# Two gather loops of a graph network on one Trainium2 core: index, edge and time loads per round of four chunks, one-hots of the first layer made in other instructions, the bound on counts tested in the setup

## The chip, the cores and the metric

The kernel runs on one core of a Trainium2 chip. The metric is the device time of one execution in microseconds (us). A core has five engines that run their own instruction streams and meet at semaphores: TensorE (PE, matrix products), VectorE (DVE), ScalarE (ACT), GpSimd (POOL, which also issues the indirect gathers here) and SyncE (SP, which issues DMAs). ACT issues DMAs too. A capital name with a q (SPq, DVEq) is the part of an engine that issues instructions.

## What is computed

Four graph layers over 6,250 nodes of 128 features and E = 206,250 edges, sorted by destination. Each layer is added to the running node features x after a normalisation. Only the first two layers and the setup are changed:

```
h = relu(layernorm(x))                      # before each layer
# layer 0: gated relational messages, one of 8 weights per edge
msg = (h @ W[rel])[src] * edge_weight1 * sigmoid((h @ g[rel])[src])
x = x + relu(segment_sum(msg, dst))
# layer 1: edge network with a time gate
ef  = (relu(attr @ We1 + be1) @ We2 + be2) * sigmoid(time * Wt + bt)
msg = relu(concat(h[src], ef) @ Wn1 + bn1) @ Wn2 + bn2
x = x + segment_sum(msg, dst) + h
# layers 2 and 3: a GRU layer and three graph convolutions, whose sums over
# edges are products with a 6250 x 6250 matrix of edge counts
```

The count matrix (how often an edge goes from node s to node d) is made beside layer 0, as bf16, for layers 2 and 3. A bf16 number holds whole counts exactly up to 256, so the kernel has a flag: if a count is larger, a branch makes the rest of the digits.

## The kernel before

Edges are padded to 206,848 = 101 rounds of NB = 4 chunks of CH = 512 edges, a chunk being J = 4 tiles of 128 edges. There are 404 chunks.

**Setup** (lines 270 to 434). SP loads destinations by row and by column, sources and edge types (lines 306 to 310); DVE finds the least destination of each chunk and its span, SP stores that as `meta` and reads it back (lines 312 to 318), DVE computes keys and, in a loop of eight (lines 412 to 423), the first and last tile of each group. The last thing is that SP stores `gout` (line 327) and reads it back as `record` (line 329).

**Layer 0** (lines 572 to 730), a software pipeline over chunks, with a loop per engine. SP copies 4 columns of `idx8`, a tile in SBUF, to a slot `staged[:, b, :]`, also in SBUF, once per chunk (line 597), as soon as the four gathers that read that slot one round earlier have landed (`rows_in[b]`, line 602). POOL waits for the slot and for `chunk_done` of four chunks earlier, and issues four indirect gathers of 128 rows of 512 bytes (line 613). DVE makes a one-hot of 4 x 64 destinations per chunk (`one_hot`, line 180); ACT multiplies it by the edge weight in place, tile by tile (`weigh_chunk`, line 688); PE multiplies rows and one-hot (line 160, four products that sum into one window), and DVE adds the window to `acc` (line 201) and raises `chunk_done` (line 225).

Into the same loops the count matrix is woven, two groups per chunk for the first 98 rounds. For each group DVE computes eight numbers (line 520) and makes four pairs of one-hots in bf16: `lo_hot` of 128 (line 516) and `hi_hot` of 392 columns (line 517), in the order lo, hi, lo, hi; PE multiplies each pair (line 549) into one of four banks; ACT copies the bank to `block_out` (line 696) and makes a second pass over it, Relu(count - 256) with a sum (line 698), into `over[:, g]`. After the layer the maximum of `over` gives the flag (lines 775 and 794 to 798).

The order on DVE in each chunk is: two sets of keys, the one-hot of the next chunk, the one-hots of two groups, then the wait for this chunk's window (`close_window`, line 206). The order on PE is: wait for rows, window product, first group, second group.

**Layer 1** (lines 938 to 1156), again a loop per engine. SP loads per chunk the 4 index columns (line 993, from `src_idx` in SBUF), and per two chunks a 256 KB piece of edge attributes from HBM (line 997). ACT issues per chunk a 256 KB load of times, broadcast to 128 partitions (line 1070). POOL gathers (line 1014). PE makes four products (lines 1041, 1047, 1059 and 160, with counts of edge types at 163), ACT makes `tw`, `hid` and `msg` (lines 1085, 1090, 1096), DVE makes `ef` (1140), `z` (1153), the one-hots (1129, 180) and adds the window (199, 201). The gather into a slot waits for `z` of four chunks earlier (line 1011).

```
                            sp.wait_ge(rows_in[b], base + 16 * J * o)
                            load(b, o * NB + b)
```

are the two lines of layer 0's loop on SP by which a slot is filled again.

## Time and profile before

| | |
|---|---|
| time, median of 3 runs | 7884.42 us (7872.66 to 7892.95) |
| profiled execution | 7896.64 us, of which 7894.2 us are the span of the trace |
| PE, DVE, ACT, POOL busy | 72%, 40%, 29%, 40% of the span |
| setup | 0 to 166 us |
| layer 0 with the count matrix | 321 to 2972 us |
| layer 1 | 3069 to 5858 us |
| layers 2 and 3 | 5858 us to the end |
| DMA | 811.20 MB in 460919 packets; 218904 of them under 512 B |

An idle stretch of an engine is printed ahead of the instruction that ended it, as [us <-what released it]. "issue" means that the trace shows nothing that the engine waited for, "remote" that a semaphore was waited for whose last increment the trace doesn't tie to an instruction that ended just then.

### The profile page before, as it was taken

Reading aid. Unit: us, or ns where it says so; the run is one execution under the profiler, and the core shown is the slowest. Engines: PE = TensorE matmul, PEld = TensorE weight load, DVE = VectorE, ACT = ScalarE, POOL = GpSimd, SP = SyncE. Lnnn points to the kernel's source line nnn. Section 1 sums busy time; section 2 is a strip of 40 time slices with the busy share of each in tenths; the row PEclk is TensorE's granted clock in tenths of the full one; section 3 lists DMA queues with packets and bytes.
Section 4 is the critical chain, followed back from the end, with each engine's and each line's share of the span. In section 5 each row is a group of like instructions: output and inputs, shape, how many; then the busy total and the mean of one; then the engine's idle time right before and its main releaser. Section 6 shows DMA issues by size and latency. Waiting matters only on the chain. (4 is left out here: it accounts for less than half of the span.)

```text
span 7894.2 us, 105906 instructions
## 1 busy us (share of the span) xinstructions
PE 5657.7 (72%) x25772; PEld 3387.9 (43%) x25773; DVE 3166.8 (40%) x11018; ACT 2317.7 (29%) x5705; POOL 3138.5 (40%) x3263
## 2 busy tenths in 40 slices
PE   0766666566666654777777777777786996999999
PEld 0333333333333433444444444444453453444444
DVE  6566666666666654333333333333322112000000
ACT  0244444444444442232222222222211112111100
POOL 0265565556665562555555555555530000000000
PEclk9856555665656556777777777777767998999999
DMA  1322222222222222333333333333313443555555
GB/s 49 147 73 73 73 72 57 73 73 73 74 73 73 69 69 72 97 96 97 94 95 96 96 95 98 95 94 97 96 53 117 157 129 131 191 173 194 172 193 162
DMA packets 460919, 811.20 MB, mean 103 GB/s; under 512 B 218904, under 2 KB 233266, under 8 KB 457671
## 3 DMA queue, kind: packets, MB, share of 16 engines
q1 hardware_dynamic: 285148, 407.76, 16.6%
q0 software_dynamic: 103968, 213.28, 10.3%
q10 hardware_dynamic: 71728, 189.18, 7.4%
q8 instruction: 45, 0.74, 0.0%
q14 instruction: 30, 0.25, 0.0%
HBM read 697.44 MB, written 110.80 MB: 102 GB/s over the span
## 5 line engine op out<-in xcount | busy, mean ns | idle before, releaser
L613 POOL DMA_INDIRECT e_rows<-scratch_table,e_staged x1616 | 1583.3, 980 | 1364.1 <-DVEq L225 607.1
L1014 POOL DMA_INDIRECT e_rows<-scratch_table,e_staged x1616 | 1533.9, 949 | 1342.5 <-DVE e_z L1153 707.6
L549 PE MATMUL e_banks<-hi_hot,lo_hot 128*128 128x392 bf16 x3138 | 1073.0, 494 | 704.4 <-remote 314.4
L517 DVE TENSOR_SCALAR hi_hot<-iota_hi,key 128x392 bf16<-128x392 f16 x3138 | 1078.9, 344 | 16.7 <-issue 16.5
L160 PE MATMUL e_win<-e_onehot,e_msg 128*128 128x64 f32 x3232 | 562.3, 332 | 663.1 <-ACT e_msg L1096 645.9
L160 PEld LDWEIGHTS e_win<-e_onehot,e_msg 128*128 128x128 f32 x3232 | 542.6, 247 | 968.7 <-ACT e_msg L1096 825.5
L160 PE MATMUL e_win<-e_onehot,e_rows 128*128 128x64 f32 x3232 | 683.6, 386 | 282.1 <-issue 212.4
L549 PEld LDWEIGHTS e_banks<-hi_hot,lo_hot 128*128 128x128 bf16 x3138 | 354.7, 132 | 1227.4 <-issue 534.0
L160 PEld LDWEIGHTS e_win<-e_onehot,e_rows 128*128 128x128 f32 x3232 | 696.4, 306 | 413.7 <-issue 366.3
L516 DVE TENSOR_SCALAR lo_hot<-iota_lo,key 128x128 bf16<-128x128 bf16 x3138 | 783.3, 250 | 193.4 <-remote 156.0
L1324 PE MATMUL c_sums<-ring,parts 128*128 128x512 bf16 (+1 forms) x3822 | 789.8, 368 | 80.9 <-DMA c_bias<-in_conv_b 80.9
L1096 ACT ACTIVATE e_msg<-e_z 128x512 f32<-128x512 f32 x404 | 254.4, 630 | 1891.3 <-DVE e_z L1153 1530.4
L1059 PE MATMUL e_p<-wn1b,e_ef 128*128 128x128 f32 x3232 | 614.4, 348 | 0.0
L1548 POOL DMA_DIRECT2D c_w<-in_convT x3 | 1.6, 534 | 1444.8 <-POOLq L65 1444.8
L1324 PEld LDWEIGHTS c_sums<-ring,parts 128*128 128x128 bf16 x3822 | 361.7, 98 | 489.9 <-DMA c_bias<-in_conv_b 81.5
L1059 PEld LDWEIGHTS e_p<-wn1b,e_ef 128*128 128x128 f32 x3232 | 520.1, 245 | 31.5 <-DVE e_ef L1140 0.9
L1047 PE MATMUL e_p<-e_hid,we 128*128 128x512 f32 x808 | 506.5, 713 | 1.1 <-ACT e_hid L1090 0.8
L1612 DVE SCALAR_TENSOR_TENSOR c_y<-c_pO,dinv,c_bias 128x128 f32<-128x128 f32 x147 | 41.6, 345 | 1118.2 <-PE c_pO L1574 1118.2
L688 ACT ACTIVATE e_onehot<-e_onehot,weight 128x64 f32<-128x64 f32 x1616 | 429.2, 342 | 149.2 <-DVE e_onehot L180 102.1
L1140 DVE SCALAR_TENSOR_TENSOR e_ef<-e_p,cols,e_tw 128x512 f32<-128x512 f32 x404 | 302.5, 749 | 389.8 <-PE e_p L1047 241.5
L698 ACT ACTIVATE excess<-e_banks,limit 128x392 bf16<-128x392 f32 x784 | 456.1, 582 | 0.0
L1153 DVE TENSOR_TENSOR e_z<-e_p,e_rows 128x512 f32<-128x512 f32 x404 | 279.4, 692 | 431.2 <-PE e_p L1059 203.7
(188 smaller groups left out, 5767.1 us busy)
## 6 DMA issues: line engine op xcount, KB each, us to landing
ring<-scratch_counts SPq DMA_DIRECT2D x336, 896.0 KB, 4.7
e_time<-in_time_rows ACTq DMA_DIRECT2D x404, 256.0 KB
e_rows<-scratch_table,e_staged POOLq DMA_INDIRECT x3232
e_edge<-in_edge_T SPq DMA_DIRECT2D x202, 256.0 KB
scratch_counts<-h ACTq DMA_DIRECT2D x12, 3136.0 KB
scratch_counts<-type_mem ACTq DMA_DIRECT2D x12, 3136.0 KB
scratch_table<-table_tile SPq DMA_DIRECT2D x49, 512.0 KB, 2.6
e_staged<-idx SPq DMA_DIRECT2D x404, 2.0 KB
```

Source lines behind the costliest of these rows:

```text
L160: last = nc.tensor.matmul(win[:, 0:W], rows[:, j, :], onehot[:, j, :], start=(j == 0), stop=(j == J - 1))
L516: nc.vector.tensor_scalar(lo_hot, iota_lo[:, :], key[:, 0:1], None, ALU.is_equal)
L517: return nc.vector.tensor_scalar(hi_hot, iota_hi[:, :], key[:, 1:2], None, ALU.is_equal)
L549: return nc.tensor.matmul(bank, lo_hot[:, slot, :], hi_hot[:, slot, :], start=start, stop=stop)
L613: pool.indirect_dma_start(rows[:, b, j, :], None, A["table0"], bass.IndirectOffsetOnAxis(ap=staged[:, b, j:j + 1], axis=0),).then_inc(rows ...
L688: last = nc.scalar.activation(onehot[:, half, j, :], onehot[:, half, j, :], ACT.Copy, scale=weight0[:, bass.ds(c * J + j, 1)])
L698: nc.scalar.activation(excess[:, k % 2, :], bank, ACT.Relu, bias=limit[:, 0:1], accum_out=over[:, bass.ds(g, 1)]).then_inc(s["flushed"], 1)
L1014: pool.indirect_dma_start(rows[:, b, j, :], None, A["table1"], bass.IndirectOffsetOnAxis(ap=staged[:, b, j:j + 1], axis=0),).then_inc(rows ...
L1047: nc.tensor.matmul(p2[:, (b - 1) % 2, :], we2[:, :], hid[:, (b - 1) % 2, :], start=True, stop=True).then_inc(s["p2"], 1)
L1059: last = nc.tensor.matmul(p3[:, (b - 2) % 2, j * P:(j + 1) * P], ef[:, (b - 2) % 2, j * P:(j + 1) * P], wn1b[:, :], start=True, stop=True)
L1140: nc.vector.scalar_tensor_tensor(ef[:, k, :], p2[:, k, :], cols1[:, 1:2], tw[:, k, :], ALU.add, ALU.mult).then_inc(s["ef"], 1)
L1324: last = nc.tensor.matmul(to, parts[part][:, bass.ds(t, 1), :], counts, start=(start and part == 0), stop=(stop and part == 2))
```

## The change

1. **Layer 0, loads.** `staged` holds two halves of 16 columns; SP fills one half per round (101 copies of 64 bytes per partition in place of 404 of 16), two rounds ahead, as soon as all four chunks of the round before last have landed. POOL waits for indexes once per round.
2. **Layer 0, edge one-hot.** DVE makes each of its four tiles in one instruction with compare and multiply; ACT's `weigh_chunk` goes.
3. **Layer 0, count matrix.** The four `lo_hot` of a group are made by one `tensor_tensor` of 512 columns ahead of the four `hi_hot`. ACT's second pass goes.
4. **The bound.** In the setup the destinations are loaded again, shifted by 256 edges (`later`), and compared: an edge whose destination equals that of the edge 256 places on sets the flag.
5. **Layer 1, loads.** SP loads per round: 16 index columns, four chunks of edges (512 KB), four chunks of times (1 MB, before on ACT's queue). The tiles for edges and times move into `h`. At the start two rounds are loaded ahead of `type_i`.

```
-            def make_pair(key, lo_hot, hi_hot):
-                nc.vector.tensor_scalar(lo_hot, iota_lo[:, :], key[:, 0:1], None, ALU.is_equal)
+            def make_lows(size, key, lo_hot):
+                return nc.vector.tensor_tensor(lo_hot, iota_lo[:, :].unsqueeze(1).to_broadcast([P, size, P]),
+                                               key[:, :, 0:1].to_broadcast([P, size, P]), ALU.is_equal)
...
+        def open_weighted_window(s, c, onehot, weight):
+            for j in range(J):
+                last = nc.vector.tensor_scalar(onehot[:, j, :], iota_w[:, :], dst_rel[:, bass.ds(c * J + j, 1)],
+                                               weight[:, bass.ds(c * J + j, 1)], ALU.is_equal, ALU.mult)
+            last.then_inc(s["onehot"], 1)
...
+                    pool.memset(later[:, :], float(2 * NP)).then_inc(s_far, 1)
...
                     sp.dma_start(rel[:, :], A["rel_cols"]).then_inc(s_rel, 16)
+                    sp.wait_ge(s_far, 1)
+                    sp.dma_start(later[0:full, :], flat_dst[LIMIT:LIMIT + full * span]
+                                 .rearrange("(p e) -> p e", e=span)).then_inc(s_later, 16)
...
                     nc.vector.tensor_copy(gout[:, 0, :], gfirst[:, :]).then_inc(s_gout, 1)
+                    dve.wait_ge(s_later, 32)
+                    nc.vector.memset(over[:, :], 0.0).then_inc(s_repeat, 1)
+                    nc.vector.tensor_tensor(repeats[:, :], dst_rows[:, :, :].rearrange("p t e -> p (t e)"), later[:, :],
+                                            ALU.is_ge).then_inc(s_repeat, 1)
+                    dve.wait_ge(s_repeat, 2)
+                    nc.vector.tensor_reduce(over[0:ROUNDS, :], repeats[:, :], AXX, ALU.max).then_inc(s_repeat, 1)
...
# layer 0, SP
-                    with sp.Fori(1, ROUNDS) as o:
-                            sp.wait_ge(rows_in[b], base + 16 * J * o)
-                            load(b, o * NB + b)
+                    def load(half, r):
+                        sp.dma_start(staged[:, half, :], idx8[:, bass.ds(r * (NB * J), NB * J)]).then_inc(index_in[half], 16)
+
+                    def reload(half, r):
                         for b in range(NB):
+                            sp.wait_ge(rows_in[b], base + 16 * J * (r - 1))
+                        load(half, r)
+                    load(0, 0)
+                    load(1, 1)
+                    reload(0, 2)
+                    with sp.Fori(1, (ROUNDS - 1) // 2) as o:
+                        reload(1, 2 * o + 1)
+                        reload(0, 2 * o + 2)
...
# layer 0, ACT
-                        nc.scalar.activation(excess[:, k % 2, :], bank, ACT.Relu, bias=limit[:, 0:1],
-                                             accum_out=over[:, bass.ds(g, 1)]).then_inc(s["flushed"], 1)
-                                if k % 2 == 0:
-                                    weigh_chunk(h * (GPH // 2) + i * NB + k // 2 + 1, (k // 2 + 1) % 2)
...
# after layer 0
-                    nc.vector.tensor_reduce(top[:, :], over[:, :], AXX, ALU.max).then_inc(s["top"], 1)
...
# layer 1, SP
+                def load(half, r):
+                    sp.dma_start(staged[:, half, :], src_idx[:, bass.ds(r * (NB * J), NB * J)]).then_inc(index_in[half], 16)
+                    sp.dma_start(edge_in[:, half, :, :], A["edge_T"][bass.ds(r * NB, NB), :, :]
+                                 .rearrange("(q a) k e -> (a k) q e", a=2)).then_inc(edges_in[half], 16)
+                    sp.dma_start(time_in[:, half, :, :].rearrange("p b e -> p (b e)"),
+                                 A["time_rows"].rearrange("(r b) e -> r (b e)", b=NB)[bass.ds(r, 1), :]
+                                 .to_broadcast([P, NB * CH])).then_inc(times_in[half], 16)
+
+                def reload(half, r):
+                    for b in range(NB):
+                        sp.wait_ge(rows_in[b], base + 16 * J * (r - 1))
...
+                    sp.wait_ge(s["p1"], (r - 1) * NB)
+                    sp.wait_ge(s["tw"], (r - 1) * NB)
+                    load(half, r)
+                load(0, 0)
+                load(1, 1)
                 sp.dma_start(type_i[:, :], A["type_cols"]).then_inc(s["type_in"], 16)
...
# layer 1, ACT
-                        load_time(c + NB - 1, b + NB - 1)
```

## Rows read from the trace of the kernel before

**Rows 1.** Busy time by stretch; columns are length, engines, PEclk, DMA share, GB/s.

```profile
166.00:321.00 155.00, 103.66 (x343) 53.60 (x343) 97.77 (x126) 37.73 (x116) 0.00 (x0) 0.96 0.42 166
321.00:2972.00 2651.00, 1677.34 (x6370) 1022.68 (x6370) 1715.24 (x7870) 1221.50 (x3968) 1583.30 (x1616) 0.59 0.24 70
3069.00:5858.00 2789.00, 2030.81 (x9696) 1355.74 (x9696) 926.42 (x2426) 808.91 (x1211) 1533.91 (x1616) 0.76 0.35 95
```

**Rows 2.** Groups by line, 321 to 2972 us: busy us, mean ns, idle before.

```profile
L613 POOL DMA_INDIRECT e_rows<-scratch_table,e_staged x1616 | 1583.3, 980 | 1364.1 <-DVEq L225 607.1 <-issue 450.6 <-DVEq L657 306.4
```

**Rows 3.** Who waited, 321 to 2972 us, DVE: total us, times, longest.

```profile
DVE acc L201 <- remote: 421.1, 152, 10.6
...
DVE lo_hot L516 <- remote: 156.0, 41, 8.4
```

**Rows 4.** Timeline of layer 0: start us, duration, instruction, idle before.

```profile
1845.17 0.21 DVE L201 TENSOR_TENSOR acc<-acc,e_win 128x64 f32 x1
...
1847.78 0.48 SPq L597 DMA_DIRECT2D e_staged<-idx  x1
...
1850.19 0.94 POOL L613 DMA_INDIRECT e_rows<-scratch_table,e_staged  x1 [0.30 <-issue]
...
1853.29 0.22 DVE L201 TENSOR_TENSOR acc<-acc,e_win 128x64 f32 x1 [3.82 <-remote]
```

**Rows 5.** Groups by line, 3069 to 5858 us.

```profile
L1014 POOL DMA_INDIRECT e_rows<-scratch_table,e_staged x1616 | 1533.9, 949 | 1342.5 <-DVE e_z L1153 707.6 <-issue 528.4 <-DMA e_staged<-src_idx 106.5
...
L1153 DVE TENSOR_TENSOR e_z<-e_p,e_rows 128x512 f32<-128x512 f32 x404 | 279.4, 692 | 431.2 <-PE e_p L1059 203.7 <-remote 139.6 <-issue 84.8
...
L199 DVE TENSOR_TENSOR type_mem<-type_mem,e_win 16x64 f32 x404 | 84.3, 209 | 836.8 <-remote 406.4 <-PE e_win L163 406.1 <-issue 24.3
```

**Rows 6.** Timeline of layer 1.

```profile
4503.88 0.49 SPq L993 DMA_DIRECT2D e_staged<-src_idx  x1
...
4504.72 0.28 SPq L997 DMA_DIRECT2D e_edge<-in_edge_T  x1
...
4505.39 0.28 PE L163 MATMUL e_win<-e_onehot,e_oh_type 128*16 128x64 bf16 x4
...
4509.28 0.21 DVE L199 TENSOR_TENSOR type_mem<-type_mem,e_win 16x64 f32 x1 [3.88 <-remote]
...
4509.83 0.69 DVE L1153 TENSOR_TENSOR e_z<-e_p,e_rows 128x512 f32<-128x512 f32 x1 [0.21 <-issue]
4510.44 0.22 DVE L1129 TENSOR_TENSOR e_oh_type<-iota_w,type_f 128x64 bf16<-128x64 f32 x1
```

**Rows 7.** Timeline of DVE in layer 0, for the spacing of starts.

```profile
1848.76 0.31 DVE L517 TENSOR_SCALAR hi_hot<-iota_hi,key 128x392 bf16<-128x392 f16 x1
1848.99 0.24 DVE L516 TENSOR_SCALAR lo_hot<-iota_lo,key 128x128 bf16<-128x128 bf16 x1
1849.15 0.31 DVE L517 TENSOR_SCALAR hi_hot<-iota_hi,key 128x392 bf16<-128x392 f16 x1
...
1854.24 0.52 DVE L180 SCALAR_TENSOR_TENSOR e_onehot<-dst_rel,neg_w,iota_w 128x256 f32<-128x256 f32 x1
1854.68 0.24 DVE L516 TENSOR_SCALAR lo_hot<-iota_lo,key 128x128 bf16<-128x128 bf16 x1
```

**Rows 8.** Timeline of the setup.

```profile
160.26 0.31 SPq L327 DMA_DIRECT2D scratch_groups<-gout  x1
...
166.09 6.69 DVE L115 TENSOR_REDUCE mean<-x 128x49 f32<-128x6272 f32 x1 [5.85 <-PEq L65]
```

**Rows 9.** Timeline of the start of layer 1.

```profile
3061.30 0.34 SPq L999 DMA_DIRECT2D type_i<-in_type_cols  x1
...
3074.57 0.93 DVE L1115 TENSOR_SCALAR type_f<-type_i 128x1616 f32<-128x1616 int32 x1
```

**Rows 10.** DMA issues of the page: line, queue, count, size of one.

```profile
e_time<-in_time_rows ACTq DMA_DIRECT2D x404, 256.0 KB
...
e_edge<-in_edge_T SPq DMA_DIRECT2D x202, 256.0 KB
```

More of the change, by code:

```diff
@@ L294, in bass_gnn @@
                                                           ("rows", "cols", "src", "rel", "x", "w"))
+                s_far, s_later, s_repeat = (sem(st, f"setup_{n}") for n in ("far", "later", "repeat"))
                 s_low, s_high, s_span, s_meta_out, s_meta_in, s_base_in, s_ready, s_id = (
@@ L531, in group_vector @@
                 dve.wait_ge(s["taken"], g + 1)
+                make_lows(PAIRS, key[:, half, :, :], lo_hot[:, half * PAIRS:(half + 1) * PAIRS, :])
                 for j in range(PAIRS):
-                    last = make_pair(key[:, half, j, :], lo_hot[:, half * PAIRS + j, :], hi_hot[:, half * PAIRS + j, :])
+                    last = make_high(key[:, half, j, :], hi_hot[:, half * PAIRS + j, :])
                 last.then_inc(s["made"], 1)
@@ L586, in bass_gnn @@
                 s = {n: sem(st, f"e0_{n}") for n in WINDOW_SEMS +
-                     ("taken", "made", "keyed", "flushed", "copied", "limit", "y_keyed", "y_made", "y_taken")}
-                index_in = [sem(st, f"e0_index{b}") for b in range(NB)]
+                     ("taken", "made", "keyed", "flushed", "y_keyed", "y_made", "y_taken")}
+                index_in = [sem(st, f"e0_index{k}") for k in range(2)]
                 stored = [sem(st, f"e0_stored{k}") for k in range(2)]
@@ L725, in _ @@
                     block_of(whole, 0, GROUPS - whole * GPH, 16 * (whole // 2))
-                    for c in range(GROUPS // 2 + 1, NC):
-                        weigh_chunk(c, c % 2)
                     act.wait_ge(stored[0], 16 * (whole // 2 + 1))
@@ L975, in run_steps @@
                     for b in range(SPR):
-                        step(o * SPR + NB + b, b, False)
+                        step(o * SPR + NB + b, NB + b, False)
                 load_meta(NC - SPR)
@@ L999, in _ @@
-                sp.dma_start(type_i[:, :], A["type_cols"]).then_inc(s["type_in"], 16)
-                for b in range(NB):
-                    load(b, b, None)
-                with sp.Fori(1, ROUNDS) as o:
-                    for b in range(NB):
-                        load(b, o * NB + b, o)
+                def load(half, r):
[5 more added lines that the diff above has]
+                                 .to_broadcast([P, NB * CH])).then_inc(times_in[half], 16)
@@ L1006, in _ @@
+                reload(0, 2)
+                with sp.Fori(1, (ROUNDS - 1) // 2) as o:
+                    reload(1, 2 * o + 1)
+                    reload(0, 2 * o + 2)
             @block.gpsimd
             def _(pool):
-                def gather(b, c, o, first):
-                    pool.wait_ge(index_in[b], o * 16 + 16)
-                    if not first:
-                        pool.wait_ge(s["z"], c - (NB - 1))
-                    pool.sem_inc(s["begun"], 1)
-                    for j in range(J):
-                        pool.indirect_dma_start(
-                            rows[:, b, j, :], None, A["table1"],
-                            bass.IndirectOffsetOnAxis(ap=staged[:, b, j:j + 1], axis=0),
-                        ).then_inc(rows_in[b], 16)
@@ L1018, in _, with one_round @@
-                for b in range(NB):
-                    gather(b, b, 0, True)
-                with pool.Fori(1, ROUNDS) as o:
-                    for b in range(NB):
-                        gather(b, o * NB + b, o, False)
+                def one_round(half, r, before, first):
+                    pool.wait_ge(index_in[half], 16 * before + 16)
+                    for b in range(NB):
+                        if not first:
+                            pool.wait_ge(s["z"], r * NB + b - (NB - 1))
+                        pool.sem_inc(s["begun"], 1)
+                        for j in range(J):
+                            pool.indirect_dma_start(
+                                rows[:, b, j, :], None, A["table1"],
+                                bass.IndirectOffsetOnAxis(ap=staged[:, half, b * J + j:b * J + j + 1], axis=0),
+                            ).then_inc(rows_in[b], 16)
@@ L1024, in _ @@
+                one_round(0, 0, 0, True)
+                with pool.Fori(0, (ROUNDS - 1) // 2) as o:
+                    one_round(1, 2 * o + 1, o, False)
+                    one_round(0, 2 * o + 2, o + 1, False)
             @block.tensor
```

112 lines of the change are left out of this document (49 added, 63 removed).

## The prediction

> **What bounds the kernel now.** I read the stages first. Layer 0 takes 2651 us and layer 1 takes 2789 us, and neither is filled by an engine: in layer 0 PE is busy for 1677, DVE for 1715 and POOL for 1583 us, in layer 1 PE for 2031 and POOL for 1534 us [rows 1]. Something waits in both, so the groups and waits come next.
>
> POOL sets the pace from below. A gather takes 0.98 us in layer 0 and the next starts 0.30 us later [rows 2, 4], so a chunk of four needs 4 x 1.28 = 5.12 us; in layer 1 it needs 4 x (0.95 + 0.30) = 5.0 us [rows 5]. For 404 chunks that is 2068 and 2020 us. Above this pace POOL waits 607.1 us for `chunk_done` of DVE in layer 0 and 707.6 us for `z` of DVE in layer 1 [rows 2, 5]. These two sums are what can be won in the loops at most.
>
> DVE in turn waits in layer 0 for "remote": 421.1 us in 152 waits ahead of the window's addition and 156.0 us in 41 waits ahead of `lo_hot`, together 577 us in 193 stalls of 3.0 us [rows 3]. In layer 1 it is 406.4 + 139.6 = 546 us [rows 5]. One stall of each layer shows what it is. In layer 0 DVE adds a window at 1845.17, has made its last one-hot at 1849.46 (4.29 us of work), and then waits 3.82 us, to 1853.29 [rows 4, 7]. POOL had issued its last gather at 1850.19. SP had issued the copy of the index columns at 1847.78, 5.5 us before the stall ends. In layer 1 the products of the window are done 0.28 us after 4505.39, but DVE gets their semaphore at 4509.28 after 3.88 us; SP had copied indexes at 4503.88, 5.4 us before [rows 6]. The same 5.4 to 5.5 us in two loops that share only this copy on SP and the gathers is my evidence that **the small copies from SBUF to SBUF hold back semaphores** that others wait for. There are 404 copies and 193 stalls in layer 0: about one stall for two copies.
>
> **The change, part by part.** The sum starts from the profiled execution, 7896.6 us.
>
> *Copies per round, layer 0.* 404 copies become 101, each still 128 rows, of 64 bytes in place of 16. Their number is taken to count, not their bytes. With one stall for each, 101 x 3.0 = 303 us of waiting remain of POOL's 607.1: **-304 us**. The bounds are 0 (the copies are not the cause) and -607 (no stall is left, POOL's own pace remains).
>
> *Copies per round, layer 1.* Likewise 202 pairs of copies, 707.6 / 202 = 3.5 us each, become 101: 354 us remain, **-354 us**, with bounds 0 and -708. The loads of times leave ACT's queue for SP's: per round 2 x 256 KB of edges and 4 x 256 KB of times follow the index copy [rows 10], 1.57 MB, at the 166 GB/s that the stretch ahead of layer 0 moved [rows 1] 9.5 us of a round of about 24 us. They are asked for a whole round ahead of their use, so a late arrival is hidden by that round. Queued behind SP's new waits (four gathers, `p1`, `tw`) is only the next round's load; PE, ACT and POOL wait for that a round later. What the bytes do to the stalls is a rival below.
>
> *The weighted one-hot.* DVE's one instruction for 4 x 64 columns is followed by the next after 0.44 us; four small ones, at the 0.16 us that `lo_hot` takes to the next start [rows 7], are 0.64 us: +0.20 us per chunk, up to +0.48 if they take 0.23 us each as `hi_hot` does. *Merged lows.* Four `lo_hot` cost 4 x 0.16 = 0.64 us. Not in the trace of before is a `tensor_tensor` of 512 bf16 columns with broadcast operands. The nearest is `z`, 512 columns, f32, next start after 0.61 us [rows 6]: -0.03 us per group. From 128 to 392 columns the fast form adds only 0.07 us, 0.27 ns per column [rows 7]; at that pace 512 columns would be 0.26 us, -0.38 per group; the other end is z's whole duration of 0.69 us, +0.05. I take z's spacing, as it too reads two tensors. DVE's work per chunk is then 4.29 + 0.20 - 0.06 = 4.43 us (3.7 to 4.9), under POOL's 5.12: **0**, hidden behind the gathers. Where that cover is gone the net 0.14 us costs 404 x 0.14 = 57 us.
>
> [...]
>
> *ACT* loses the weighing (a hop between DVE and PE) and the second pass over every bank. It was busy for 1222 of 2651 us [rows 1] and its share is not the pace; banks come free earlier. 0 taken, a few us either way.
>
> *Setup.* A further 0.8 MB on SP's queue goes ahead of the store of `meta`; at 166 GB/s [rows 1] it is 5 us: **+5** (0 to +8), since DVE's next step waits for that round trip. On POOL a fill of 2048 columns goes first, beside loads that last far longer. DVE's comparison and maximum of 2048 columns, at z's spacing of 0.61 us for 512 [rows 6], take 2.4 us each. They run after `gout`, while SP stores and reads back the groups, from 160.26 to DVE's next start at 166.09 [rows 8]: hidden; 4.8 us if not. The reduction left out after layer 0 saves about 1 us; 0 taken.
>
> *Start of layer 1.* `type_i` now waits behind two rounds of loads, 3.1 MB, at 166 GB/s 19 us; it is issued at 3061.30 and used at 3074.57, 13 us later, with two fills of DVE in between [rows 9]. About **+8** (0 to +15).
>
> Sum: 7896.6 - 304 - 354 + 5 + 8 = 7252 us. The median of the runs is 12 us below the profiled execution, so the forecast is **7240 us**.
>
> **The rivals.**
>
> *The stalls go altogether.* If a round's copy is issued while there is slack, POOL is four chunks ahead and never notices: -607 - 708 in place of -304 - 354, 6583 us; with a part of the slack, anything from there to 7100. For it: DVE's 4.43 us is below 5.12 us, so a lag could be made up, at 0.7 us per chunk about as much as a stall of 3 us costs in four chunks. [...]
>
> *The stall grows in layer 1.* The 1 MB of times and the edges follow the copy on the same queue. If the stall lasts as long as the queue's transfers, 7.0 us in place of 3.5 us, one stall costs as much as two did, and the layer gains nothing: 7240 + 354 = 7594 us. For it: 9.5 us of transfer per round. Against: the edge load of 256 KB, issued 0.84 us behind the copy, doesn't lengthen that stall beyond 5.4 us, what layer 0 shows without one [rows 4, 6]. [...]
>
> *The copies are not the cause, and DVE becomes the bound of layer 0.* Then the remote waits stay, and what DVE does in a chunk lies on the path: ahead of each wait for PE's semaphore stands +0.20 us for the one-hot and, at the upper end, +0.05 us for each of the two merges. At the lower value, without a gain from the merge, 404 x 0.20 = 81 us, with setup and start 94 us: 7884 + 94 = 7978 us. It decides from the point where the copies' gain in both layers is under 94 us. For it: gathers, too, are in flight in each stall, and their traffic doesn't change. Against: the 5.4 us.
>
> *Nothing that can be told from no change*, 7884 us: gains and costs cancel.
>
> **How the numbers follow.** The forecast, one stall per round, 0.45 (its own range 7100 to 7400); stalls gone in good part, below 7100, 0.20; layer 1 without gain, 7400 to 7650, 0.20; slower, about 7980, 0.10; no change, 0.05. About 0.3% is what a measurement of this kernel can tell from no change. The range 6650 to 7650 leaves out the last two and the lowest end of the second, under 0.2 together. Faster 0.85, same 0.05, slower 0.10.
>
> **What would show it.** Right: in layer 0 the remote waits of DVE halve, to about 100 stalls and 300 us, POOL's wait for `chunk_done` to about 300 us, and each stall that is left ends some 5.4 us after a copy on SP; the like in layer 1 with `z` and 354 us. If POOL's wait falls under 100 us, the first rival holds. If layer 1's stalls are few but 7 us long, the second. If their number stays near 193 and 404 chunks take over 2651 us, the third. The merged lows should start 0.6 us ahead of the first `hi_hot`, the setup should end 5 us later. The prediction is most wrong if the number of copies is not what counts but, say, what they read or who issues them.

## The result

The changed kernel takes **7753.1 us** (median of 4 runs, 7751.8 to 7755.9), the kernel before 7880.4 us (4 runs, 7872.7 to 7893.0). The ratio is 0.9835 with a 95% interval of 0.9823 to 0.9846: 127 us faster, where 640 were forecast, and outside of the range, which ended at 7650. The profiled execution of the changed kernel has a span of 7749.6 us; all its rows here come from it.

There is a second result, which the first measurement could not show. The experiments ran on several chips. On two of them (before: 7839 and 7915 us) the kernel before takes about as long as on the first, and the kernels profiled there with all their gathers have the same waits. On four others the kernel before takes 6593 to 6597 us, and there **the changed kernel is slower**: 6752.1 us against 6595.0, ratio 1.0237 (1.0220 to 1.0254). What parts the two kinds in the traces is the wait that they call "remote": every kernel with all its gathers has it on the one kind, and none has it on the other. I call them chips with and without stalls. Each ratio below is to the kernel before on the same chip. That the chip decides is not shown: only one of them was used at two times (without stalls at both), and one of ten runs of `lo32`, on a chip where the other nine took 6598 to 6613 us at a granted clock of 0.85, took 7833 us at 0.63; it has no trace, and it is left out of what follows.

The stretches of the changed kernel, on the first chip (columns as in [rows 1]: length, busy time of PE, PEld, DVE, ACT, POOL, granted clock, DMA share, GB/s):

```profile
168.00:324.00 156.00, 102.27 (x343) 52.90 (x343) 98.28 (x125) 37.69 (x116) 0.00 (x0) 0.97 0.41 165
324.00:2853.00 2529.00, 1557.37 (x6371) 937.07 (x6371) 1791.45 (x6732) 381.59 (x784) 1749.24 (x1616) 0.66 0.24 73
2950.00:5738.00 2788.00, 2035.12 (x9789) 1355.47 (x9790) 916.88 (x2426) 775.22 (x1210) 1524.97 (x1607) 0.77 0.30 94
```

Compared with [rows 1], the gain lies in layer 0, which went from 2651 to 2529 us. Layer 1, where 354 us were forecast, stays (2789 and 2788). One column moved that nothing in the prediction moves: POOL's busy time in layer 0, 1583 to 1749 us for the same 1616 gathers. These are POOL's groups, to be compared with [rows 2] and [rows 5]. The columns are busy us, mean ns, and idle time before by what ended it; the first row is layer 0, the second layer 1:

```profile
L647 POOL DMA_INDIRECT e_rows<-scratch_table,e_staged x1616 | 1749.2, 1082 | 1074.1 <-issue 477.0 <-DVEq L693 308.2 <-DVEq L232 288.9
```

```profile
L1045 POOL DMA_INDIRECT e_rows<-scratch_table,e_staged x1607 | 1525.3, 949 | 1215.8 <-DVE e_z L1174 722.6 <-issue 493.2
```

In layer 0 POOL waits 289 us for `chunk_done` (DVEq L232) where it waited 607, so the 304 us that were forecast for its waiting are there, nearly to the number; but each gather takes 1082 ns where it took 980, and that gives 166 us back. In layer 1 the wait for `z` is 723 us after and 708 before: there are a quarter of the copies and the same waiting.

DVE's waits for remote, layer 0 and layer 1 (total us, times, longest):

```profile
DVE acc L208 <- remote: 221.6, 111, 7.3
DVE lo_hot L542 <- remote: 99.4, 45, 8.1
```

```profile
DVE type_mem L206 <- remote: 404.0, 91, 8.3
...
DVE e_z L1174 <- remote: 253.7, 102, 4.2
```

In layer 0 they fell from 577 to 321 us [rows 3], in layer 1 they rose from 546 to 658 [rows 5]. The stall itself can be seen where no copy is near. The timeline of layer 0 of the changed kernel:

```profile
1811.01 0.95 POOL L647 DMA_INDIRECT e_rows<-scratch_table,e_staged  x1 [0.30 <-issue]
1812.27 0.94 POOL L647 DMA_INDIRECT e_rows<-scratch_table,e_staged  x1 [0.30 <-issue]
...
1818.54 0.94 POOL L647 DMA_INDIRECT e_rows<-scratch_table,e_staged  x1 [0.30 <-issue]
```

```profile
1797.77 24.00 SPq L626 DMA_DIRECT2D e_staged<-idx  x2
```

```profile
1821.28 0.49 SPq L626 DMA_DIRECT2D e_staged<-idx  x1
```

```profile
1814.29 1.08 PE L161 MATMUL e_win<-e_onehot,e_rows 128*128 128x64 f32 x8 [2.80 <-issue]
```

```profile
1812.83 0.98 DVE L196 TENSOR_SCALAR e_onehot<-iota_w,dst_rel,weight 128x64 f32<-128x64 f32 x4
1813.73 0.68 DVE L542 TENSOR_TENSOR lo_hot<-iota_lo,key 128x512 bf16<-128x512 bf16 x1
1814.33 1.00 DVE L546 TENSOR_SCALAR hi_hot<-iota_hi,key 128x392 bf16<-128x392 f16 x4
...
1820.68 0.22 DVE L208 TENSOR_TENSOR acc<-acc,e_win 128x64 f32 x1 [3.82 <-remote]
```

PE has finished the window at 1815.37. DVE gets to know at 1820.68, 5.3 us later. SP issued one copy at 1797.77 and the next at 1821.28 (the first row groups the two, the second has the later one), 17.6 us before PE's last product and 0.6 us after the stall: none is issued in between. What is under way from 1811.01 to 1819.5 are seven gathers, one behind the other. In the kernel before, SP waited for the landing of gathered rows to issue its copy, and I had read the distance between copy and stall as a cause. It was read off one stall of each layer, and the whole trace of the kernel before does not have it as a rule. Of the 193 stalls of layer 0, counted there, 35 end 5.2 to 5.7 us after a copy was issued, and 122 end less than 1 us after one, too soon for that copy to have begun them; in layer 1 it is 83 of 227 that end at 5.2 to 5.7 us.

### The profile page after: what moved, and what is told of

Its sections match the earlier page's. It is cut to its first block and busy times, and to the rows that moved or that the text cites. A ratio compares the mean times of both kernels' runs of the same rounds, so it can differ in the third digit from the quotient of the medians.

```text
span 7749.6 us, 97114 instructions
## 1 busy us (share of the span) xinstructions
PE 5526.1 (71%) x25772; PEld 3281.9 (42%) x25773; DVE 3241.6 (42%) x9879; ACT 1444.4 (19%) x2521; POOL 3306.1 (43%) x3264
## 5 line engine op out<-in xcount | busy, mean ns | idle before, releaser
L647 POOL DMA_INDIRECT e_rows<-scratch_table,e_staged x1616 | 1749.2, 1082 | 1074.1 <-issue 477.0
L1045 POOL DMA_INDIRECT e_rows<-scratch_table,e_staged x1616 | 1533.8, 949 | 1316.3 <-DVE e_z L1174 722.6
L580 PE MATMUL e_banks<-hi_hot,lo_hot 128*128 128x392 bf16 x3138 | 983.9, 458 | 625.6 <-DVE hi_hot L546 340.6
L161 PE MATMUL e_win<-e_onehot,e_rows 128*128 128x64 f32 x3232 | 635.0, 364 | 355.5 <-issue 185.0
L161 PEld LDWEIGHTS e_win<-e_onehot,e_rows 128*128 128x128 f32 x3232 | 629.8, 282 | 492.9 <-issue 326.3
L546 DVE TENSOR_SCALAR hi_hot<-iota_hi,key 128x392 bf16<-128x392 f16 x3138 | 800.0, 316 | 0.0
L580 PEld LDWEIGHTS e_banks<-hi_hot,lo_hot 128*128 128x128 bf16 x3138 | 313.9, 121 | 1108.1 <-issue 617.1
L542 DVE TENSOR_TENSOR lo_hot<-iota_lo,key 128x512 bf16<-128x512 bf16 x786 | 536.1, 682 | 167.1 <-remote 99.4
L1072 PE MATMUL e_p<-h,we 64*128 64x512 f32 x808 | 347.8, 951 | 139.0 <-issue 119.4
L1345 PE MATMUL p3S<-ring,parts 128*128 128x512 bf16 (+1 forms) x1911 | 393.7, 368 | 68.7 <-DVE emb L1482 68.7
L206 DVE TENSOR_TENSOR type_mem<-type_mem,e_win 16x64 f32 x404 | 84.3, 209 | 811.1 <-remote 404.0
```

Of the source, the lines that this page charges most:

```text
L161: last = nc.tensor.matmul(win[:, 0:W], rows[:, j, :], onehot[:, j, :], start=(j == 0), stop=(j == J - 1))
L542: return nc.vector.tensor_tensor(lo_hot, iota_lo[:, :].unsqueeze(1).to_broadcast([P, size, P]), key[:, :, 0:1].to_broadcast([P, size, P]), ...
L546: return nc.vector.tensor_scalar(hi_hot, iota_hi[:, :], key[:, 1:2], None, ALU.is_equal)
L580: return nc.tensor.matmul(bank, lo_hot[:, slot, :], hi_hot[:, slot, :], start=start, stop=stop)
L647: pool.indirect_dma_start(rows[:, b, j, :], None, A["table0"], bass.IndirectOffsetOnAxis(ap=staged[:, half, b * J + j:b * J + j + 1], axis=0),
L1045: pool.indirect_dma_start(rows[:, b, j, :], None, A["table1"], bass.IndirectOffsetOnAxis(ap=staged[:, half, b * J + j:b * J + j + 1], axis=0),
```

## The experiments

Two theories stand against each other. COPIES is the prediction's: SP's small copies hold semaphores back. GATHERS: gathers in flight do it. A third, PORT, is about the 166 us of longer gathers: VectorE's comparisons hold POOL up.

**Twice the copies.** The suspected cost doubled:

```diff
 sp.dma_start(staged[:, b, :], idx8[:, bass.ds(c * J, J)]).then_inc(index_in[b], 16)
+sp.wait_ge(spare_in[b], 16 * o)
+sp.dma_start(spare[:, b, :], idx8[:, bass.ds(c * J, J)]).then_inc(spare_in[b], 16)
```

> The kernel before, with every per-chunk index copy on SP's queue issued a second time into a buffer that nobody reads (some 800 copies more in the two edge layers). Two theories. COPIES (the prediction's): the small copies on SP's queue hold back what TensorE reports; then twice as many would cost about what taking three quarters of them away was forecast to bring, 300 us or more, so 8200 us or later. GATHERS: TensorE's semaphore increments are held back while gathered rows are landing, and the copies only happened to be issued at that moment, since SP waits for the rows; then the second copies cost nothing, 7860 to 7910 us, and the acc wait for remote in layer 0 stays near 421 us.

6597.7 us, ratio 1.0001 (0.9992 to 1.0011). But the chip has no stalls, so this says that 808 more copies cost nothing there, not what they do on the other kind. It cannot settle the theories, and neither can the next two experiments, from the same chip.

**The loads per round, one layer at a time,** the kernel before otherwise:

> The kernel before with the index loads per round in layer 0 alone. COPIES: -300 us by the prediction, 7580 us. GATHERS: within 30 us of before; the 134 us that layer 0 gained in the whole change then come from the other parts (the weighing taken from ScalarE, the second pass taken off, the one-hots in another order).

> The kernel before with the loads per round of four chunks in layer 1 alone. COPIES: -350 us by the prediction, 7530 us. GATHERS: the copies are not the cause, so within 30 us of before, 7850 to 7910 us; the comparison of the two traces had layer 1 at 2772 to 2752 us.

Layer 0 alone: 6597.5 us, 1.0001 (0.9992 to 1.0011). Layer 1 alone: 6585.8 us, 0.9983 (0.9974 to 0.9993). The first moves nothing, the second some 10 us. On this chip there is nothing else to win, as POOL's group of `l0_only` shows (first layer 0, then layer 1):

```profile
L618 POOL DMA_INDIRECT e_rows<-scratch_table,e_staged x1616 | 1600.7, 991 | 795.9 <-issue 468.2 <-DVEq L666 303.7 <-DVEq L225 24.1
L1023 POOL DMA_INDIRECT e_rows<-scratch_table,e_staged x1616 | 1543.8, 955 | 594.4 <-issue 469.4 <-DMA e_staged<-src_idx 113.1 <-DVE e_z L1162 11.9
```

POOL waits 24 us for `chunk_done` where it waited 607 [rows 2] and 12 us for `z` where it waited 708 [rows 5]. It gathers without a break, from 318.9 to 2410.9 us in layer 0 and from 2514.0 to 4549.1 us in layer 1: POOL is the bound of both edge layers on a chip without stalls.

**One gather of four.** The kernel before, all of SP's copies kept, with only gather 0 of each chunk; three quarters of the rows stay zero, so that part of the sums is left out.

```diff
-for j in range(J):
+for j in range(1):
     pool.indirect_dma_start(rows[:, b, j, :], None, A["table0"], ...)
```

The arguments behind `...` are left out here. Not shown: the same in layer 1, the waits for rows at a quarter of their counts, and one fill of the rows with zeros ahead of each layer.

> The kernel before, with only the first of the four gathers of each chunk in both edge layers; the other three quarters of the rows stay zero, so the output is not the reference's. SP's copies are untouched. COPIES: the stalls stay, as each copy is still there: the waits for remote of VectorE stay near 700 us in layer 0 and 608 us in layer 1, and layer 1, which is not bound by GpSimd, stays at about 2790 us. GATHERS: the waits for remote fall to a quarter or less of that (under 150 us in each layer), layer 0 goes to VectorE's pace, 4.4 us a chunk or some 1850 us, and layer 1 falls by 300 us or more.

> The kernel before with one of four gathers of each chunk (the other rows stay zero, so the output is not the reference's), once more for a chip with waits for remote. There GATHERS: under 300 us of such waits on VectorE, and within 150 us of 6260 us. COPIES: the waits stay near 1190 us. On a chip without them: 6260 us, nothing told.

On three chips without stalls it took 6258, 6261 and 6260 us (one_gather, one_gather_2, one_gather_3), which tells only how much POOL's pace costs there. The fourth run met a chip with stalls, on which the kernel before took 7915 us (7 runs): **6261.4 us**, ratio 0.7912. That is the time of the other chips. DVE's waits in both edge layers of that run, 322 to 4210 us:

```profile
DVE type_mem L199 <- PE e_win L163: 323.5, 399, 1.6
DVE e_z L1157 <- PE e_p L1063: 269.5, 399, 1.7
DVE e_ef L1144 <- PE e_p L1051: 236.3, 221, 2.1
...
DVE acc L201 <- PE e_win L160: 22.6, 12, 4.1
```

No row of it says remote, and the waits for PE are no longer than 4.1 us, where single stalls had been up to 10.6 [rows 3]. On the same chip `skew`, described below, has 454 us of waits for remote in layer 0 alone. All 808 index copies are there. GATHERS holds and COPIES falls: the stalls need the gathers in number, a kernel with a quarter of them has none, and in layer 1 of the changed kernel a quarter of the copies left the waiting whole. Whether it is POOL's issuing of the gathers or the rows themselves on their way that holds semaphores back, this does not tell, as both went.

**The one-hots.** The changed kernel again on a chip without stalls, and four edits of it.

> The changed kernel itself, beside the kernel before on the chip of these experiments. On the chip of the first measurement, whose trace has 1190 us of waits for remote, it was 130 us faster than before (0.9835). Here the kernel before takes 6595 us and its traces have no wait for remote at all. COPIES: with no stall to remove nothing is left of the gain, and what is left is the removed weighing on ScalarE and its way to TensorE, 0.98 to 1.00. GATHERS: the copies never mattered, and the gain of 134 us in layer 0 came from the one-hots; GpSimd sets the pace of layer 0 here (1616 gathers of 980 ns), and the merged one-hots lengthen its gathers to 1082 ns, so no faster than before, 6550 to 6700 us.

> The changed kernel with the narrow one-hots not merged: for each tile the 128-wide and then the 328-wide comparison, as before. The prediction has the two forms equal (0.61 against 0.64 us a group). Theory PORT: four of the wide comparisons back to back hold GpSimd out of memory it shares with VectorE, and lengthen the gathers beside them; with the pairs back the mean gather of layer 0 falls from 1082 ns to about 980 ns, and the kernel is faster than the changed one by 60 to 160 us. Rival: the mean gather stays above 1050 ns and the time is the changed kernel's within 20 us.

The edit (the wide comparison has 392 columns, the 328 of that text is a slip):

```diff
-make_lows(PAIRS, key[:, half, :, :], lo_hot[:, half * PAIRS:(half + 1) * PAIRS, :])
 for j in range(PAIRS):
+    nc.vector.tensor_scalar(lo_hot[:, half * PAIRS + j, :], iota_lo[:, :], key[:, half, j, 0:1], None, ALU.is_equal)
     last = make_high(key[:, half, j, :], hi_hot[:, half * PAIRS + j, :])
```

> As the changed kernel, but the merged comparison is split into its four narrow comparisons, still ahead of the four wide ones. It tells the order from the form. PORT by order (wide comparisons back to back are what hurts): mean gather as in the changed kernel, near 1080 ns, in layer 0. PORT by form (the merged tensor-tensor comparison is what hurts): near 980 ns, as with the pairs.

> The changed kernel with the layer-0 node one-hot made by one VectorE comparison and weighed on ScalarE again, as before. The prediction put the change of this at +0.20 us a chunk of VectorE, hidden, 0 in the time. Theory: what the changed kernel gained in layer 0 comes from the way VectorE, ScalarE, TensorE that this puts back into each chunk (two semaphores less), so this is slower than the changed kernel by 50 to 130 us; rival: within 20 us of it, with the gain in the second pass over the counts.

The edit of `weigh_act` puts back `weigh_chunk` of the kernel before, word for word. The group of the gathers of layer 0 in each, in the order after_again, pairs, lows_first, weigh_act:

```profile
L647 POOL DMA_INDIRECT e_rows<-scratch_table,e_staged x1616 | 1767.1, 1093 | 801.1 <-issue 469.6 <-DVEq L693 308.9 <-DVEq L232 22.6
```

```profile
L647 POOL DMA_INDIRECT e_rows<-scratch_table,e_staged x1616 | 1698.4, 1051 | 800.9 <-issue 469.0 <-DVEq L693 308.8 <-DVEq L232 23.2
```

```profile
L648 POOL DMA_INDIRECT e_rows<-scratch_table,e_staged x1616 | 1804.8, 1117 | 800.4 <-issue 474.2 <-DVEq L694 308.2 <-DVEq L232 18.0
```

```profile
L650 POOL DMA_INDIRECT e_rows<-scratch_table,e_staged x1616 | 1647.9, 1020 | 802.2 <-issue 459.2 <-DVEq L696 310.1 <-DVEq L235 32.9
```

| kernel | time, us | ratio | POOL busy, layer 0 | first to last gather |
|---|---|---|---|---|
| l0_only (one-hots of before) | 6597.5 | 1.0001 | 1600.7 | 2092.0 |
| weigh_act | 6637.4 | 1.0063 | 1647.9 | 2139.2 |
| pairs | 6689.2 | 1.0141 | 1698.4 | 2189.6 |
| after_again | 6752.1 | 1.0237 | 1767.1 | 2258.3 |
| lows_first | 6790.4 | 1.0295 | 1804.8 | 2296.1 |

The last column is the one before it plus 491 us, in every row within 1 us. So **on a chip without stalls layer 0 lasts as long as its gathers, and what the one-hot edits cost is what they add to the gathers**. No other engine is needed to explain it: 1767.1 - 1600.7 = 166 us longer in POOL, 157 us longer in all. Undoing the merge gives 63 us back, undoing the weighing on DVE 115; together that is more than the 157, so the two do not simply add. lows_first kept the four narrow comparisons apart, yet bundled, and is the slowest: with these the order, not only the merged form, matters.

Several of the expectations missed. The changed kernel is slower than either theory had it (6700 us at most). `pairs` gained the 63 us at the low end of its range, but its mean gather fell to 1051 ns only, not to 980. `weigh_act` was expected to be slower than the changed kernel by 50 to 130 us and is faster by 115.

**Without the wide comparisons.** I had `hi_hot` in suspicion, four in a row:

> The changed kernel without the wide comparisons of layer 0: their tile is filled with zeros once, so the counts, and with them the output, are not the reference's; all else is issued as before. It tells whether these comparisons are what lengthens the gathers beside them. Theory PORT: every gather of layer 0 takes its 944 ns, beside the merged narrow comparison, the weighted slices and the window sums too, and on a chip without waits for remote layer 0 takes 1616 x (0.944 + 0.29) = 1994 us, against 2258 us in the changed kernel and 2092 us before: 6490 us in all. Rival: some other instruction beside them does it, then the mean stays above 1000 ns. On a chip with waits for remote: the mean falls likewise, and layer 0 keeps its waits for remote of 220 us or more.

6704.7 us, 1.0165 (1.0136 to 1.0195), mean gather 1060 ns, not 944: my theory had the wrong instruction, or at least not all of them. The timeline of DVE and POOL of that kernel shows another:

```profile
1000.05 1.04 DVE L196 TENSOR_SCALAR e_onehot<-iota_w,dst_rel,weight 128x64 f32<-128x64 f32 x4
1000.09 0.94 POOL L647 DMA_INDIRECT e_rows<-scratch_table,e_staged  x1 [0.30 <-issue]
...
1000.95 1.28 DVE L542 TENSOR_TENSOR lo_hot<-iota_lo,key 128x512 bf16<-128x512 bf16 x2
1001.34 1.72 POOL L647 DMA_INDIRECT e_rows<-scratch_table,e_staged  x1 [0.30 <-issue]
```

The gather beside the weighted slices takes its 0.94 us. The next is issued at 1001.34, within the first of two merged comparisons that end at 1002.23, and takes 1.72 us. The same is seen in the changed kernel on the first chip; this gather starts 0.31 us before a merged comparison ends:

```profile
1822.56 0.69 DVE L542 TENSOR_TENSOR lo_hot<-iota_lo,key 128x512 bf16<-128x512 bf16 x1
1822.94 1.35 POOL L647 DMA_INDIRECT e_rows<-scratch_table,e_staged  x1 [0.31 <-issue]
```

What counts is what DVE runs when a gather starts. This table sorts the 1616 gathers of layer 0 by that, worked out from the traces (number of gathers and their mean in ns; a narrow comparison is `lo_hot`, merged in the last two columns, a wide one `hi_hot`):

| DVE at the gather's start | l0_only | woven_2 | pairs | weigh_act | after_again |
|---|---|---|---|---|---|
| idle, keys or window sum | 496, 944 | 271, 944 | 478, 944 | 687, 944 | 500, 944 |
| edge one-hot | 84, 1050 | 328, 989 | 245, 953 | 136, 1068 | 358, 1003 |
| narrow comparison | 160, 1012 | 260, 956 | 500, 1164 | 437, 1172 | 637, 1275 |
| wide comparison | 876, 1007 | 757, 1013 | 393, 1099 | 356, 961 | 121, 1025 |

In `after_again` the gathers that start in a merged comparison make up 211 of the 242 us by which all gathers exceed 944 ns. In `weigh_act` they make up 100 us, and this difference of 111 us is nearly all of the 119 us between the two in POOL's busy time. The merged comparison is the same in both; with the weighing back on ScalarE fewer gathers start in it, and each of them loses less (0.23 us in place of 0.33). So an edit of DVE's instructions costs by where it lets the gathers fall among them. Why they fall where they do, and why one start costs more than another, the traces do not settle.

In `after_again` the 637 gathers that start in a merged comparison, which reads two tiles, take 1.275 us in the mean, against 0.944 us for those that start while VectorE is idle, at its keys or at a window sum; the one of 1.72 us above takes 0.78 us more than that. What such a gather waits for, no run shows; that it is held out of memory, as theory PORT has it, is my guess. In the other direction no such delay is seen. In the changed kernel on the first chip 664 of the 786 merged comparisons start while a gather is under way, and they take 682 ns in the mean, the 122 others 685. In the timeline under the result a gather starts first, and a merged comparison in the middle of it takes its usual 0.68 us:

```profile
1814.76 0.94 POOL L647 DMA_INDIRECT e_rows<-scratch_table,e_staged  x1 [0.30 <-issue]
1815.26 0.68 DVE L542 TENSOR_TENSOR lo_hot<-iota_lo,key 128x512 bf16<-128x512 bf16 x1
```

The four weighted slices cost most gathers beside them nothing: of the 358 that start in one in `after_again`, the median is 944 ns.

**The order.** The same instructions as in `pairs`, with the four slices put one by one behind every second pair (the edit in short, not word for word):

```diff
 for j in range(PAIRS):
     lo_hot(j); hi_hot(j)
+    if j % 2 == 1:
+        one weighted slice of the next node one-hot
```

> The changed kernel with pairs again and with the four weighted slices of the node one-hot put one by one behind every second pair, in place of four in a row ahead of the groups: the same instructions of VectorE as in the kernel called pairs, in another order. If what lengthens a gather is an unbroken run of two-byte comparisons beside it, the slices (beside which a gather took 944 ns) break the run, and the mean gather falls below that kernel's 1052 ns towards 1000 ns: 6610 to 6650 us on a chip without waits for remote. If only the total time of such comparisons counts, the mean stays at 1050 ns and the time at 6690 us.

> The kernel called woven again, to have it on a chip without waits for remote: there its gathers, 986 ns beside the pairs in its first run, give layer 0 1616 x (0.98 + 0.29) = 2052 to 2090 us, and 6575 to 6620 us in all, faster than the kernel called pairs (6689) by 70 us or more. On a chip with such waits again 0.992 of before.

```profile
L649 POOL DMA_INDIRECT e_rows<-scratch_table,e_staged x1616 | 1595.7, 987 | 799.4 <-issue 467.2 <-DVEq L695 307.3 <-DVEq L232 25.0
```

6587.0 us, 0.9987 (0.9977 to 0.9996): 102 us faster than `pairs` by order alone, through the gathers again (1051 to 987 ns), as the expectations had it or a little more. That an unbroken run of comparisons is what lengthens them is not shown, though: `l0_only` has the same eight pairs in one unbroken run, and its gathers take 991 ns. By the table above its 1036 gathers that start in a comparison take 1008 ns in the mean, the 893 of `pairs` take 1135. What sets the moments at which gathers start is open. On chips without stalls this kernel beats the one before and the changed one, the first by little. On a chip with stalls (its first run) it took 7772.0 us, 0.9918 (0.9901 to 0.9935); the changed kernel's 0.9835 is from another such chip.

**The form.**

> The kernel called pairs_act with the narrow comparisons read from four-byte numbers in place of two-byte ones, as the weighted slices are, beside which a gather took 944 ns. If two-byte comparisons hold GpSimd off and four-byte ones do not, the time for which it is held off falls by the narrow ones' share (0.16 of 0.39 us a pair), the mean gather to 960 to 970 ns, and layer 0 by 20 to 50 us: 6540 to 6570 us on a chip without waits for remote. If the form does not matter, the mean stays near that of before, 990 ns, and the time at 6575 to 6595 us. On a chip with such waits: within 20 us of pairs_act's 0.991 of before.

6607.2 us (nine runs), 1.0018 (1.0008 to 1.0028), mean gather 1003 ns, where 960 to 970 were expected if two bytes were what hurts. Four bytes in `lo_hot`'s input bring no gain. `pairs_act`, which differs by this alone, ran only on a chip with stalls, so how the two compare is not shown.

**The rest of the change.** First with both one-hot edits undone, then ScalarE's part alone:

> The changed kernel with both one-hot edits of layer 0 undone: the narrow and wide comparisons alternate, and ScalarE weighs the node one-hot. What is left of the change are the loads per round, the bound on the counts taken once in the setup, and ScalarE's second pass taken off. On a chip without waits for remote: the single steps measured 63 us (pairs) and 115 us (weighing on ScalarE) against the changed kernel's 6752 us; if they add up, 6575 us, 0.997 of before, with a mean gather near 990 ns in layer 0. If the gathers' mean alone sets layer 0 and the second pass is worth nothing, 6590 us. On a chip with waits for remote as in the first traces: if the gain of 130 us came with the loads or the second pass it is all here (7750 us), if it came with the weighing it is gone (7880 us).

> The kernel before with one part of the change alone: ScalarE's second pass over each bank taken off, and the counts bounded once in the setup instead. The prediction gave it 0 and 5 us for the setup. On a chip with waits for remote pairs_act, which has this and the loads per round, was 69 us faster than before: if the pass is what brings that (each bank is free 0.58 us sooner), 0.990 to 0.993 here, and the loads bring nothing; if the loads do, within 0.2 per cent of before. On a chip without such waits, where GpSimd sets layer 0's pace, no gain either way; but if a bank that is free sooner lets VectorE run its comparisons without a break, and these then lie beside more of the gathers, the mean gather rises from 990 ns to over 1000 ns and the time to 1.001 to 1.005 of before.

`pairs_act` met a chip with stalls: 7769.8 us, 0.9912 (0.9892 to 0.9933), 69 us faster than before, with remote waits of 461 us on DVE in layer 0 and POOL's wait for `chunk_done` at 471 us. The expectation had all of the gain here or none, and it is about half:

```profile
DVE acc L211 <- remote: 297.8, 116, 10.4
...
DVE lo_hot L565 <- remote: 162.8, 61, 6.8
```

`no_pass` met one without: 6602.3 us, 1.0008 (0.9999 to 1.0018). There the pass is worth nothing. Which of the pass and the loads brings the 69 us where there are stalls is not known.

**A sum one chunk late.** If the stalls cost through the way from PE's window to DVE's add, two banks for the window and a later add should hide them:

```diff
-pe.wait_ge(s["added"], o * NB + b + 1)
-pe.wait_ge(s["chunk_done"], o * NB + b + NB)
+late = 1 if b else 0
+pe.wait_ge(s["added"], o * NB + b + 1 - late)
+pe.wait_ge(s["chunk_done"], o * NB + b + NB - late)
```

> The kernel called woven, with the window sum of layer 0 in two banks, and VectorE adding three of four of them one chunk late, so that neither it nor TensorE waits for the other's last step within a chunk. On a chip without waits for remote GpSimd sets layer 0's pace, so nothing: 6575 to 6600 us. On a chip with them, where acc waited 168 us for remote in woven and the way from window to sum is what each stall lengthens: layer 0 shorter by 60 to 250 us than woven's 2657 us (first gather to first gather), 0.96 to 0.985 of before. If the stalls hit every later wait alike, no gain there either, 0.99.

On a chip with stalls, 8009.1 us, **1.0128** (1.0111 to 1.0144), where 0.99 was the worst expected: slower than before and, by ratio, than `woven`. DVE's waits in layer 0 of `woven`, on the chip where before takes 7839 us, and then of `skew`, on that of 7915 us:

```profile
DVE lo_hot L562 <- remote: 193.6, 100, 4.0
DVE acc L208 <- remote: 164.4, 75, 11.9
```

```profile
DVE lo_hot L562 <- remote: 390.6, 128, 5.9
...
DVE acc L208 <- remote: 63.3, 19, 10.5
```

The wait of `acc` went from 164 to 63 us as meant, but that of `lo_hot` from 194 to 391, and POOL's for `chunk_done` from 482 to 718 us. One wait was hidden and another grew, as far as two chips with stalls can be compared. That it got slower I put down to `chunk_done`, which now comes after the next chunk's keys, so that POOL gets its buffer later; no run shows this by itself.

## Why the prediction was wrong

- *The bound.* The reading of the bound was right: POOL's pace below, its waits of 607 and 708 us above it as what can be won. Chips without stalls confirm it: with the stalls gone these waits are 24 and 12 us.
- *The cause of the stalls.* **This is the step that failed, and it carried 658 us, more than the whole gain that was forecast.** "The small copies from SBUF to SBUF hold back semaphores" rested on one distance, 5.4 us, read at one stall in each of two loops; the same trace has it at 35 of 193 stalls and 83 of 227. The prediction named the gathers as the other thing that both loops share and did not ask which of the two is there in stalls without the other. Layer 1 gave nothing of its 354 us (waits for remote 546 to 658 us), and one_gather_4 removed every stall with every copy in place. The second rival had layer 1 without gain, but by 101 stalls of 7 us; it has 193 of 3.4 us in the mean. Whether the larger loads made them longer (2.4 us before) was not tested by itself.
- *Layer 0's 304 us.* The signs came out nearly to the number by luck: POOL's wait fell by 318 us, to 289, and DVE's waits for remote to 321 us, though in 156 stalls and not 100. Copies per round can't be it alone, as layer 1 shows. With both one-hot edits undone 69 us of gain are left on another chip with stalls; the rest of the 127 came with them, though the same edits cost 157 us where there are no stalls. A possible reading is that gathers that start further apart hold back less, as the waits for remote fell from 577 to 321 us when the gathers became longer. No run takes that by itself, and it stays open.
- *The weighted one-hot.* Forecast 4 x 0.16, up to 0.92 us; in the timeline above it is 0.90 us (1812.83 to 1813.73), +0.46 a chunk, at the upper end. *The merged lows*: forecast 0.61, measured 0.60 us (1813.73 to 1814.33). Both sizes within their bounds, and DVE did stay under POOL's pace.
- *"0, hidden behind the gathers."* The second step that failed. DVE's time was hidden, but the cover itself grew: the gathers that were to hide it became 102 ns longer each in layer 0, 166 us. The prediction costed DVE's instructions by their time on DVE only. The third rival had the cause of the stalls open, as it should be, and made the kernel slower by 94 us through DVE. On the chip of the forecast that did not come about; where there are no stalls the kernel is 157 us slower, through POOL.
- *ACT, 0.* Right where there are no stalls (no_pass, 1.0008); open where there are.
- *Setup, +5.* The reduction behind the setup starts at 171.3 us, it was 166.1 [rows 8]: +5.2, right; the first gather starts at 325.2 us, it was 321.6, so 3.6 of it are left there. *Start of layer 1, +8.* From the last gather of layer 0 to the first of layer 1 it is 99.0 us, it was 107.5 (2961.7 to 3069.2): 8.5 less; the first `z` follows its first gather after 17.4 us in place of 12.8. Together -4 in place of +8.
- *The range.* It was built from bounds of one cause, and rival three, the cause being another, was given 0.10. The chance of "no gain from the copies" should have been near one half, since what spoke for them spoke for the gathers as well.

## What to carry to other kernels

A distance between two events that is read at one place is no cause: count it over all the stalls of the trace, and look for a stall without the suspect beside it and for the suspect without a stall. Here VectorE's work fitted beside GpSimd's gathers, which set the pace, and was not free: a gather of layer 0 took 1082 ns in place of 980 on the first chip, 1093 (after_again) in place of 992 (before_twice) without stalls. In such a kernel read the duration of the gathers before and after, not VectorE's busy time, and try the same instructions in another order before giving an edit up. Where a tuning gain rests on stalls that only some chips showed, measure on both kinds, as it can be a loss on the other: the same change gave 0.9835 here on the one kind and 1.0237 on the other.

## What the runs showed of the hardware

- The same program took 6595 us on some chips and 7839 to 7915 us on others, and the difference lies in the two edge layers. From first to last gather, layer 0 takes 2640 us in the kernel before on the first chip and 2094 in `before_twice` on one without stalls, layer 1 takes 2769 and 2034; DVE's waits for remote are 577 and 608 us against none. What lies behind the last gather takes 2056 and 2045 us. Why some chips have these stalls is open.
- TensorE's clock was granted higher in the runs without stalls. In the kernel before the mean is 0.59 and 0.76 of full speed in the two layers [rows 1], which is the level of 0.5 for 82% and 49% of the time, with PE busy for 63% and 73% of them. In `before_twice`, without stalls, it is 0.74 and 0.91, the level of 0.5 for 52% and 17%, with PE busy for 66% and 82%; in one_gather_4, on a chip with stalls, 0.84 and 0.92, with PE busy for 70% and 85%:

```profile
322.00:2150.00 1828.00, 1273.05 (x6362) 803.12 (x6362) 1613.01 (x7865) 1219.52 (x3964) 413.24 (x402) 0.84 0.18 58
2255.00:4205.00 1950.00, 1651.65 (x9596) 1081.96 (x9595) 916.17 (x2403) 803.39 (x1203) 382.63 (x404) 0.92 0.34 95
```

- A gather that starts while VectorE is idle, or at its keys or a window sum, takes 0.944 us in the mean in all five kernels of the table; those that start in a merged comparison take 1.275 us in the mean in `after_again`, and one of them took 1.72 us in `no_wide`. The order of VectorE's instructions alone was worth 64 ns for each of 1616 gathers (1051 in `pairs`, 987 in `woven_2`).
